# Attention context in 64-column tiles with whole transposes, in a fused language-model tower on one core

## The chip, the cores and the metric

The kernel runs on one core of a Trainium2 chip. The core's engines are TensorE (PE; its weight loads are listed apart as PEld), VectorE (DVE), ScalarE (ACT), GpSimd (POOL) and the DMA queues, here fed by SyncE (SP). The metric is the device time of one execution in microseconds (us), the median of several runs. Lower is better.

## The reference

Sixteen sequences of 128 tokens go through one transformer layer. A token adds only its bracket level (0 to 31) to the model, so a row of the input is one of 32 rows of a table:

```python
levels = _compute_levels(token_ids, 32)         # scan with clip over 128 tokens
h = level_emb[levels] * 0.15                    # 16 x 128 x 256
x = layernorm(h)
q = x @ Wq + bq          # 16 heads of 16
k, v = x @ Wk + bk, x @ Wv + bv                 # 4 key heads, repeated 4 times
attn = softmax(q @ k.T / 4)                     # no mask
h = h + (attn @ v) @ Wo + bo
...
Wq1, Wq2 = quantize(W1), quantize(W2)           # ternary: clip(round(W / mean|W|), -1, 1)
h = h + relu(layernorm(h) @ Wq1.T + b1) @ Wq2.T + b2     # 1024 hidden columns
```

## The kernel before, in words

Two rows of one sequence with the same level are equal, so everything is computed once for each of 32 levels in each of 16 sequences: 512 rows, as four **groups** g = 0 to 3 of four sequences (4 x 32 = 128 rows). Which level occurs how often in a sequence weights the softmax. In the names, `BG` is 4 (sequences in a group), `H2` is 2, `D` 256, `KVD` 64 and `VW` 68 (64 value columns and 4 columns for the sums of the four key heads).

The stages are these.

1. The levels: tokens are compared, a scan (`level_scan`) makes levels, `level_ends`, `end_codes` and `gone_levels` find the highest and lowest level of each sequence, `end_columns` (line 623, tile `endx`) spreads them for a matmul, `level_onehot` makes the one-hot `oh`.
2. Scores of the table: keys (`ktm`, split in a rounded part `khi` and a rest `klo`) and queries (`qs`, written by `query_hi` on ACT and `query_lo` on DVE). `scores` (lines 949, 950) makes the 128 x 128 table of scores; `prefix_max` (two scans), `prefix_t` (line 955, two transposes), `maxima`, `max_hi` and `max_parts` (tile `ms`) make from it the row maxima of each sequence. `scores_t(g)` writes the transposed scores of group g into its PSUM bank `psg[g]`, and `less_max` (line 980, 16 matmuls) subtracts the maxima.
3. Attention: `exps(g)` on ACT makes `et`; `values` on DVE makes `vo`, and POOL multiplies it by the counts to `voc`, one instruction a group (line 392). `context(g)` (line 988): four matmuls, one a sequence, each with 128 columns of `et` as weights and 68 columns of `voc` moving. The 128 columns are the four query heads of a key head by 32 levels, in two halves `a` of 64. `inverse_sums(g)` and `normalise(g)` divide (`cn`, DVE). `context_t(g)` (line 997): sixteen small transposes of 64 x 64 pieces as eight matmuls against an identity. `ctx_out(g)` copies them to `cT` (ACT), `out_proj(g)` (line 1006) multiplies by Wo, `add_table(g)` adds the residual (`hq`).
4. The second layernorm: `row_stats`, `row_moments`, `variance_eps` (DVE), a power on POOL (line 400) for two groups at once, `norm_rows` (ACT), `rows_t` (line 1012, two transposes a group), `x_hi` (ACT) and `x_lo` (DVE), which split in a rounded part and a rest.
5. Feed-forward: the weights are made ternary on the way: `magnitudes(w, i)` (ACT, line 442) and `signs(w, i)` (DVE, line 703, and one quarter on POOL, line 386), a sum on PE (`abs_total`), `threshold(w)`, `ternary(w, q)` (DVE, line 720), `weights_t(u)` (PE, line 1046) and `weights_out(u)` (ACT). `ffn1(h, j)` (line 1064, four matmuls of 256 columns) makes 128 hidden columns j of the two groups of half h; `hidden` (ACT) and `hidden_lo` (DVE) apply relu and split; `ffn2(j, g)` (line 1079, two matmuls) adds them up for group g; `final(g)`, `spread(g)` (line 1098), `result(g)` and the output DMAs follow.

Every engine runs a list of such steps that is written out by hand, and waits on semaphores; there is no scheduler. `keep_warm(n)` (line 884) are n matmuls of zeroes that only fill TensorE's time. SP issues all loads at the start in one order, and the outputs at the end.

The order of the lists is what ties the engines together. On PE before:

```python
less_max()
keep_warm(5, psmisc[0])
weights_t(0)
context(0)
context(1)
context_t(0)
weights_t(1)
context_t(1)
out_proj(0)
out_proj(1)
```

## Time and profile before

| | |
|---|---|
| median of 3 runs | 58.94 us (58.08 to 59.61) |
| the profiled execution | 58.45 us |
| its span, first to last instruction | 56.6 us |
| granted TensorE clock, mean over the span | 0.975 |
| PE busy | 49.2 us (87%), 416 records |
| DVE busy | 42.0 us (74%) |
| ACT busy | 31.2 us (55%) |
| POOL busy | 19.8 us (35%) |

A matmul of 32-bit type in its full precision stands as two records in the trace, and so do its weight loads. A busy PE is not PE at its peak: records overlap, so the pace is read from one start to the next and not from the durations. The profiled execution lasts 1.85 us longer than its span.

### The profile page before, as it was taken

How to read it: one execution, taken by the hardware profiler on the slowest of the kernel's cores; microseconds unless marked ns; L12 is line 12 of the kernel's file. 1: busy time of each engine (PE TensorE's matmuls, PEld its weight loads, DVE VectorE, ACT ScalarE, POOL GpSimd, SP SyncE). 2: the span in 40 equal slices, each digit the busy share in tenths (PEclk: the TensorE clock that was granted, in tenths of full speed). 3: DMA queues.
4: the chain of work that ended last, by engine and by line, in shares of the span. 5: the costliest groups of instructions: out<-in, count | busy, mean ns of one | idle time of the engine just before them, and what ended most of it. 6: DMA issues, size and time to landing. Idle time of an engine off the chain costs nothing.

```text
span 56.6 us, 1236 instructions
## 1 busy us (share of the span) xinstructions
PE 49.2 (87%) x416; PEld 38.7 (68%) x416; DVE 42.0 (74%) x140; ACT 31.2 (55%) x73; POOL 19.8 (35%) x36
## 2 busy tenths in 40 slices
PE   1999999899996969996699999999999999998300
PEld 0333797546875958895479899989999688994000
DVE  4998739999699999699199987955659599347400
ACT  0585007832129916950980897989796958106100
POOL 5935089998049920009900000695000000000000
PEclk9999999999999999999999999999999999999955
DMA  0363899986520000000000000000000009730594
GB/s 0 67 204 55 159 260 411 417 333 148 131 76 12 12 0 0 0 0 0 0 12 0 0 0 0 0 0 0 6 0 0 12 5 364 255 116 0 210 383 148
DMA packets 4658, 5.37 MB, mean 95 GB/s; under 512 B 1117, under 2 KB 4141, under 8 KB 4653
## 3 DMA queue, kind: packets, MB, share of 16 engines
q1 hardware_dynamic: 4602, 5.28, 29.3%
q8 instruction: 3, 0.05, 0.3%
q10 hardware_dynamic: 51, 0.02, 0.1%
q14 instruction: 2, 0.02, 0.1%
HBM read 3.21 MB, written 2.10 MB: 94 GB/s over the span
## 4 chain that ended last, share of the span: by engine, by line
PE 66%; DVE 16%; issue 5%; ACT 3%; POOL 2%; DVEq 0%; POOLq 0%
PE pswt L1064 15%; PE psmisc L1079 14%; PE psg L880 6%; PE psg L1006 5%; DVE tern L720 5%; PE psg L1098 5%; PE psg L997 4%; PE psg L1012 3%; PE psg L884 2%; PE psg L1046 2%; POOL rs L400 2%; PE psg L967 2%; DVE hq L744 1%; DVE st L748 1%; PE psg L972 1%
## 5 line engine op out<-in xcount | busy, mean ns | idle before, releaser
L478 ACT ACTIVATE hr<-pswt,b1c 128x256 f32<-128x256 f32 x16 | 7.6, 473 | 2.8 <-PE pswt L1064 2.5
L1079 PE MATMUL psmisc<-w2T,hh 128*128 128x256 f32 x32 | 8.4, 292 | 0.0
L1079 PE MATMUL psmisc<-w2T,hl 128*128 128x256 f32 x32 | 8.0, 281 | 0.0
L1064 PE MATMUL pswt<-xhi,w1T 128*128 128x256 f32 x32 | 7.1, 303 | 0.0
L771 DVE TENSOR_TENSOR hl<-hr,hh 128x256 fp32r<-128x256 f32 x16 | 6.4, 424 | 0.7 <-ACT hh L480 0.3
L720 DVE SCALAR_TENSOR_TENSOR tern<-aw,thr,sg 128x512 bf16<-128x512 f32 x8 | 6.5, 842 | 0.0
L1064 PE MATMUL pswt<-xlo,w1T 128*128 128x256 f32 x32 | 6.4, 281 | 0.0
L1079 PEld LDWEIGHTS psmisc<-w2T,hh 128*128 128x128 f32 x32 | 6.1, 190 | 0.3 <-DVE hl L771 0.3
L400 POOL TENSOR_TENSOR rs<-ve,mhalf 128x2 f32<-128x2 f32 x2 | 1.7, 871 | 12.6 <-DVE ve L756 12.6
L1079 PEld LDWEIGHTS psmisc<-w2T,hl 128*128 128x128 f32 x32 | 6.1, 190 | 0.0
L1064 PEld LDWEIGHTS pswt<-xhi,w1T 128*128 128x128 f32 x32 | 5.0, 190 | 0.6 <-ACT hr L478 0.3
L1064 PEld LDWEIGHTS pswt<-xlo,w1T 128*128 128x128 f32 x32 | 4.9, 189 | 0.0
L392 POOL TENSOR_TENSOR voc<-vo,cpos 128x272 f32<-128x272 f32 x4 | 3.8, 966 | 2.5 <-DVE vo L694 2.5
L880 PE MATMUL psg<-warm 128*128 128x512 bf16 x8 | 3.6, 631 | 1.2 <-DVE tiny L547 1.2
L442 ACT ACTIVATE aw<-w 128x1024 f32<-128x1024 f32 x4 | 4.2, 1053 | 0.2 <-DMA w<-in_L_ffn_W_dram 0.2
L1006 PE MATMUL psg<-wo,cT 128*128 128x256 f32 x16 | 4.2, 392 | 0.0
L485 ACT ACTIVATE aw<-psg 128x256 f32<-128x256 f32 x6 | 2.0, 384 | 3.9 <-PE psg L1098 3.9
L988 PE MATMUL psg<-voc,et 128*128 128x68 f32 x32 | 4.0, 274 | 0.0
L988 PEld LDWEIGHTS psg<-voc,et 128*128 128x128 f32 x32 | 3.8, 192 | 0.0
L386 POOL TENSOR_SCALAR sg<-w 128x1024 bf16<-128x1024 f32 x1 | 3.6, 3642 | 0.0
L776 DVE TENSOR_TENSOR fin<-psmisc,hb 128x256 f32<-128x256 f32 x4 | 1.7, 423 | 2.5 <-PE psmisc L1079 2.5
L781 DVE COPY aw<-psg 128x256 f32<-128x256 f32 x7 | 2.7, 420 | 1.1 <-PE psg L1098 1.1
(166 smaller groups left out, 114.5 us busy)
## 6 DMA issues: line engine op xcount, KB each, us to landing
w<-in_L_ffn_W_dram SPq DMA_DIRECT2D x4, 512.0 KB, 6.0
out_dram<-aw SPq DMA_DIRECT2D x8, 256.0 KB, 2.3
wq<-in_L_attn_Wq_dram SPq DMA_DIRECT2D x1, 256.0 KB, 3.1
wo<-in_L_attn_Wo_dram SPq DMA_DIRECT2D x4, 64.0 KB
emb<-in_L_tok_level_emb_dram SPq DMA_DIRECT2D x1, 128.0 KB
bo_bc<-in_L_attn_bo_dram SPq DMA_DIRECT2D x1, 128.0 KB, 8.3
b_bc<-in_L_ffn_b_dram SPq DMA_DIRECT2D x1, 128.0 KB, 7.0
wk<-in_L_attn_Wk_dram SPq DMA_DIRECT2D x1, 64.0 KB, 2.4
```

Source lines behind the costliest of these rows:

```text
L386: nc.gpsimd.tensor_scalar(sg[:, 0, 0:1024], halves(0, 0), 0.0, 0.5, ALU.is_ge, ALU.subtract).then_inc(g_sgn, 1)
L392: nc.gpsimd.tensor_tensor(voc[:, bs, :], vo[:].unsqueeze(1).to_broadcast([P, BG, VW]), cpos[:, bs].unsqueeze(2).to_broadcast([P, BG, VW]), ...
L400: nc.gpsimd.tensor_tensor(rs2[:, c], ve2[:, c], mhalf[:].to_broadcast([P, HALF]), ALU.pow).then_inc(g_rs2, 1)
L442: nc.scalar.activation(aw[:, w, i * 1024:(i + 1) * 1024], halves(w, i), ACT.Abs, accum_out=asum[:, 2 * w + i:2 * w + i + 1]).then_inc(a_ab ...
L478: nc.scalar.activation(hr[:, n % NHR, :], pswt[n % 2][:, 0:RH], ACT.Relu, bias=b1c[:, j:j + 1]).then_inc(a_hr, 1)
L720: V.scalar_tensor_tensor(tern[:, w, c], aw[:, w, c], thr[:, w:w + 1], sg[:, w, c], ALU.is_gt, ALU.mult).then_inc(v_tern, 1)
L771: V.tensor_tensor(hl[:, n, :], hr[:, n % NHR, :], hh[:, n, :].bitcast(F32), ALU.subtract).then_inc(v_hl, 1)
L880: mm(bank[:, :], warm[:, 0:P], warm[:], start=True, stop=True)
L988: ins = mm(psg[g][:, b * VW:(b + 1) * VW], et[:, g, b, :], voc[:, g * BG + b, :], start=True, stop=True)
L1006: ins = mm(psg[g][:, 0:D], cT[:, g, e].rearrange("p b l -> p (b l)"), wo[:, e, :], start=(e == 0), stop=(e == H2 - 1))
L1064: ins = mm(pswt[n % 2][:, 0:RH], w1T[:, j, k, :], part[:, k, HALF * h:HALF * (h + 1), :].rearrange("p g n -> p (g n)"), start=(m == 0 and ...
L1079: ins = mm(psmisc[r][:, 0:D], part[:, n, r * P:(r + 1) * P], w2T[:, j, :], start=(j == 0 and m == 0), stop=(j == FC - 1 and m == 1))
```

## The change

There are three parts.

- `context(g)` makes the context of two sequences together: the weights are 64 columns of `et` (half `a` of one sequence), and the output of the two sequences t = 0, 1 of a pair goes to partitions 0 to 63 and 64 to 127 of the same columns. Eight matmuls a group in place of four, each with half of the weight columns and again 68 moving columns. The sums and the product by their inverse (`inverse_sums`, `normalise`) are as before.
- With this layout, `context_t(g)` is two whole 128 x 128 transposes in place of eight matmuls on 64 x 64 pieces, and `ctx_out(g)` reorders while it copies.
- The lists of PE, DVE and ACT have a new order. POOL's and SP's are the same.

```diff
             def ctx_out(g):
                 act.wait_ge(p_cT, g + 1)
-                nc.scalar.activation(cT[:, g].rearrange("p e b l -> p (e b l)"), psg[g][:, 0:D], ACT.Copy).then_inc(a_cT, 1)
+                nc.scalar.activation(cT[:, g], psg[g][:, 0:D].rearrange("p (b e l) -> p e b l", b=BG, e=H2), ACT.Copy).then_inc(a_cT, 1)
...
             def context(g):
                 pe.wait_ge(g_voc, g + 1)
                 pe.wait_ge(a_exp, g + 1)
-                for b in range(BG):
-                    ins = mm(psg[g][:, b * VW:(b + 1) * VW], et[:, g, b, :], voc[:, g * BG + b, :], start=True, stop=True)
+                for pair in range(H2):
+                    for a in range(2):
+                        c = (2 * pair + a) * VW
+                        for t in range(2):
+                            b = 2 * pair + t
+                            ins = mm(psg[g][64 * t:64 * t + 64, c:c + VW], et[:, g, b, 64 * a:64 * a + 64], voc[:, g * BG + b, :],
+                                     start=True, stop=True)
                 ins.then_inc(p_ctx, 1)
 
             def context_t(g):
                 pe.wait_ge(v_cn, g + 1)
-                dst = psg[g][:, 0:D].rearrange("p (e b l) -> p b e l", e=H2, b=BG)
-                for b in range(BG):
-                    for a in range(2):
-                        q = slice(64 * a, 64 * a + 64)
-                        ins = mm(dst[q, b], cn[q, g, b * KVD:(b + 1) * KVD], identf[q, q], start=True, stop=True)
+                for pair in range(H2):
+                    ins = nc.tensor.transpose(psg[g][:, pair * P:(pair + 1) * P], cn[:, g, pair * P:(pair + 1) * P], identf[:])
                 ins.then_inc(p_cT, 1)
```

Of the lists the diff shows two places on PE; `keep_warm` matmuls go from 27 to 22.

```diff
             less_max()
-            keep_warm(5, psmisc[0])
             weights_t(0)
+            abs_total(1)
             context(0)
             context(1)
+            context(2)
             context_t(0)
```

Three places are shown as they stand in the programs. First, **DVE from the keys to the prefix maxima**, in the first quarter. Before, from `key_blocks` (`ktm`) on:

```order
L637 SCALAR_TENSOR_TENSOR ktm<-psmisc,bkc,km 128x128
L628 TENSOR_SCALAR above<-jlev,ends 16x128
L631 SCALAR_TENSOR_TENSOR gone<-jlev,ends,above 16x128
L616 SCALAR_TENSOR_TENSOR ends<-ends 16x1 x2
L643 CAST khi<-ktm 128x128
L653 TENSOR_TENSOR qs<-psg,qs 64x2x32
L647 TENSOR_TENSOR klo<-ktm,khi 128x128
L653 TENSOR_TENSOR qs<-psg,qs 64x2x32
L623 TENSOR_SCALAR endx<-sele,ends 16x128 x2
L660 TENSOR_SCALAR oh<-pswt,pnum 128x256
L683 SCALAR_TENSOR_TENSOR pmx<-reset,psmisc 128x128
L660 TENSOR_SCALAR oh<-pswt,pnum 128x256
```

After, from `gone_levels` (`above`) on:

```order
L628 TENSOR_SCALAR above<-jlev,ends 16x128
L631 SCALAR_TENSOR_TENSOR gone<-jlev,ends,above 16x128
L637 SCALAR_TENSOR_TENSOR ktm<-psmisc,bkc,km 128x128
L623 TENSOR_SCALAR endx<-sele,ends 16x128 x2
L643 CAST khi<-ktm 128x128
L653 TENSOR_TENSOR qs<-psg,qs 64x2x32 x2
L647 TENSOR_TENSOR klo<-ktm,khi 128x128
L660 TENSOR_SCALAR oh<-pswt,pnum 128x256
L675 SCALAR_TENSOR_TENSOR top<-pswt,pnum,bm 128x128
L660 TENSOR_SCALAR oh<-pswt,pnum 128x256
L683 SCALAR_TENSOR_TENSOR pmx<-reset,psmisc 128x128 x2
```

`gone_levels` and the end codes move ahead of the keys, `endx` moves from behind `klo` and `qs` to ahead of `khi`, and both scans (`pmx`) follow each other, where the second stood one row below the piece shown and `oh` between them.

Second, **DVE from the maxima to the first two contexts**. Before:

```order
L699 SCALAR_TENSOR_TENSOR ms<-mhi,lowrow,psmisc 128x128
L707 TENSOR_SCALAR gam<-pswt 128x2
L710 TENSOR_TENSOR thr<-gam 128x1
L690 COPY cpos<-pswt 128x16
L691 TENSOR_TENSOR vo<-pswt,bm 128x64
L694 COPY vo<-bm 128x4
L720 SCALAR_TENSOR_TENSOR tern<-aw,thr,sg 128x512
L686 TENSOR_SCALAR ident<-ridx 128x128
L720 SCALAR_TENSOR_TENSOR tern<-aw,thr,sg 128x512 x2
L725 RECIPROCAL rec<-psg 128x16
L730 TENSOR_TENSOR cn<-psg,rec 128x256
```

After:

```order
L720 SCALAR_TENSOR_TENSOR tern<-aw,thr,sg 128x512
L699 SCALAR_TENSOR_TENSOR ms<-mhi,lowrow,psmisc 128x128
L690 COPY cpos<-pswt 128x16
L691 TENSOR_TENSOR vo<-pswt,bm 128x64
L694 COPY vo<-bm 128x4
L686 TENSOR_SCALAR ident<-ridx 128x128
L703 TENSOR_SCALAR sg<-w 128x1024
L720 SCALAR_TENSOR_TENSOR tern<-aw,thr,sg 128x512 x2
L725 RECIPROCAL rec<-psg 128x16
L707 TENSOR_SCALAR gam<-psmisc 128x2
L710 TENSOR_TENSOR thr<-gam 128x1
L730 TENSOR_TENSOR cn<-psg,rec 128x256
```

The first ternary (`tern`) moves ahead of `ms`; `sg` of the second weights stands between the identity and the next two ternaries, and the second threshold (`gam`, `thr`) and `eb` stand among the normalisations.

Third, **PE up to the first feed-forward matmul**, from the third context before and from the fourth one after. Before:

```order
L988 MATMUL psg<-voc,et 128x68 x4
L1021 MATMUL psmisc<-asum,ones 128x2
L1046 MATMUL pswt<-ident,tern 128x128 x4
L884 MATMUL psmisc<-warm 128x256
L988 MATMUL psg<-voc,et 128x68 x4
L1012 MATMUL psg<-identf,xn 128x128 x2
L997 MATMUL psg<-identf,cn 64x2x32 x8
L1012 MATMUL psg<-identf,xn 128x128 x2
L997 MATMUL psg<-identf,cn 64x2x32 x8
L1006 MATMUL psg<-wo,cT 128x256 x2
L1064 MATMUL pswt<-xhi,w1T 128x256 x2
```

After:

```order
L992 MATMUL psg<-voc,et 64x68 x8
L999 MATMUL psg<-identf,cn 128x128 x2
L1048 MATMUL pswt<-ident,tern 128x128 x8
L1008 MATMUL psg<-wo,cT 128x256 x2
L999 MATMUL psg<-identf,cn 128x128 x2
L1048 MATMUL pswt<-ident,tern 128x128 x4
L884 MATMUL psmisc<-warm 128x256
L1014 MATMUL psg<-identf,xn 128x128 x4
L1008 MATMUL psg<-wo,cT 128x256 x2
L884 MATMUL psmisc<-warm 128x256 x2
L1066 MATMUL pswt<-xhi,w1T 128x256 x2
```

`context(2)` now stands ahead of this place. The transposes of groups 2 and 3 (L997, now L999) and the product by Wo of group 2 (L1006, now L1008) move ahead of the normalised rows (L1012, now L1014); that of group 3, which stood among the feed-forward matmuls, stands right behind them.

Among the ACT steps, `magnitudes(1, 0)` moves ahead of `max_hi` and `magnitudes(1, 1)` ahead of the exponentials; both stood behind them.

## Rows read from the trace of the kernel before

**Rows 1.** The page: busy time, share of the span and instructions of each engine.

```profile
PE 49.2 (87%) x416; PEld 38.7 (68%) x416; DVE 42.0 (74%) x140; ACT 31.2 (55%) x73; POOL 19.8 (35%) x36
```

**Rows 2.** Stretch 30.50 to 50.80: busy time (x instructions) of each engine, PEclk, DMA.

```profile
30.50:50.80 20.30, 20.30 (x175) 18.56 (x173) 14.73 (x44) 14.67 (x36) 3.10 (x5) 1.00 0.15 53
```

**Rows 3.** The chain that ended last: start us, us, what.

```profile
11.50 0.23 PE psg L967
...
15.43 0.35 DVE ms L699
...
19.88 0.43 DVE cn L730
...
24.45 0.38 DVE st L748
...
25.08 0.16 DVE ve L756
...
33.48 0.86 PE psg L1006 x4
...
50.76 0.68 PE psg L1098 x8
```

**Rows 4.** Timeline 7.9 to 12: start us, us, engine line op [idle before <-releaser].

```profile
7.95 0.35 DVE L637 SCALAR_TENSOR_TENSOR ktm<-psmisc,bkc,km 128x128 f32<-128x128 f32 x1 [1.22 <-issue]
8.21 2.06 POOL L382 TENSOR_SCALAR sel<-jdx,pnum 128x512 fp32r<-128x512 int32 x1
...
9.15 0.21 DVE L643 CAST khi<-ktm 128x128 fp32r<-128x128 f32 x1
...
9.97 0.23 DVE L653 TENSOR_TENSOR qs<-psg,qs 64x64 fp32r<-64x64 f32 x1
10.25 3.64 POOL L386 TENSOR_SCALAR sg<-w 128x1024 bf16<-128x1024 f32 x1
10.34 0.30 PE L949 MATMUL psmisc<-khi,qs 128*128 128x128 f32 x1 [0.28 <-DVE qs L653]
...
11.52 0.48 DVE L660 TENSOR_SCALAR oh<-pswt,pnum 128x256 fp32r<-128x256 f32 x1
```

**Rows 5.** Line 623, both instructions: duration ns min/median/max.

```profile
L623 DVE TENSOR_SCALAR endx<-sele,ends x2: 234/666/1099, 10.2 to 11.2; 16x128 bf16<-16x128 bf16 x2
```

**Rows 6.** Timeline of TensorE at the prefix transposes.

```profile
13.12 0.38 PE L955 MATMUL psmisc<-identf,pmx 128*128 128x128 f32 x2
```

**Rows 7.** Tile w, the feed-forward weights: durations ns min/median/max; time to landing.

```profile
L442 ACT ACTIVATE aw<-w x4: 1047/1053/1060, 9.3 to 22.3; 128x1024 f32<-128x1024 f32 x4
...
DMA to landing us min/median/max: 4.6/6.0/7.1
```

**Rows 8.** Timeline of TensorE, VectorE and GpSimd, 15.8 to 20.4.

```profile
15.89 0.67 PE L980 MATMUL psg<-ms,sel 32*128 32x128 f32 x16
16.24 0.74 DVE L720 SCALAR_TENSOR_TENSOR tern<-aw,thr,sg 128x512 bf16<-128x512 f32 x1
16.42 3.75 POOL L392 TENSOR_TENSOR voc<-vo,cpos 128x272 f32<-128x272 f32 x4 [2.53 <-DVE vo L694]
...
17.49 2.19 DVE L720 SCALAR_TENSOR_TENSOR tern<-aw,thr,sg 128x512 bf16<-128x512 f32 x2
17.89 1.95 PE L988 MATMUL psg<-voc,et 128*128 128x68 f32 x16
...
20.36 0.68 PE L997 MATMUL psg<-identf,cn 64*64 64x64 f32 x16 [0.52 <-DVE cn L730]
```

**Rows 9.** Timeline of GpSimd: the two power instructions.

```profile
25.38 1.04 POOL L400 TENSOR_TENSOR rs<-ve,mhalf 128x2 f32<-128x2 f32 x1 [5.20 <-DVE ve L756]
...
35.75 0.70 POOL L400 TENSOR_TENSOR rs<-ve,mhalf 128x2 f32<-128x2 f32 x1 [7.37 <-DVE ve L756]
```

**Rows 10.** Timeline of TensorE at the first normalised rows.

```profile
27.46 0.44 PE L1012 MATMUL psg<-identf,xn 128*128 128x128 f32 x2 [1.08 <-ACT xn L464]
...
30.20 0.59 PE L1064 MATMUL pswt<-xhi,w1T 128*128 128x256 f32 x2
```

175 lines of the change are left out of this document (87 added, 88 removed).

## The prediction

> **What bounds the kernel now.** I read the page first. TensorE (PE) is busy for 49.2 of 56.6 us and DVE for 42.0 [rows 1]. That is an average, so I went on to single stretches. From 30.5 to 50.8 us PE has no idle time at all, while DVE and ACT are busy for 14.7 us of the 20.3 [rows 2]: this is feed-forward work that stands in PE's queue, and only less of it or an earlier start shortens it. The chain of waits agrees: it reaches the last spreads at 50.76 over PE alone [rows 3]. Before 30 us the chain changes engines. It goes over the row maxima (`ms`, 15.43), the ternaries, the first context divided (`cn`, 19.88) and the moments of the second layernorm (`ve`, 25.08) to the normalised rows on PE at 27.46, before which PE stood idle for 1.08 us [rows 3, 10]. So there are two currencies. What comes off DVE's chain before 25.2 makes the feed-forward start earlier, and what comes off PE's queue behind 27.46 makes it start earlier or last less. Work taken off PE before that is worth only what waits for it.
>
> **The new matmuls.** Two old contexts are 16 records in 1.95 us [rows 8]. A record lasts 0.27 (two transposes 0.11 apart take 0.38 [rows 6]), so starts are (1.95 - 0.27) / 15 = 0.112 apart, 0.9 us for the 8 of a group. With only 68 moving columns the load of 128 weight columns can be what sets this pace. The new form has 16 records of half the weights for each group. The nearest row is the old transpose: 64 x 64 pieces with 64 moving columns, 16 records a group in 0.68 us, by the same reading 0.03 apart, 0.46 a group [rows 8]. Bounds for a new context are therefore 0.46 us (pairs run together), 0.9 (half the load, no pairs) and 1.8 (each record as slow as now). I take 0.5, since the row with the same weight columns and nearly the same moving columns shows it. For contexts 0 to 2 this hardly counts: POOL makes one `voc` in 0.94 us on average, four in 3.75 [rows 8], and each context must wait for its own. Two whole transposes, 0.11 apart, are 0.22 and replace 0.46, so 0.25 is saved a group, 1.0 us in all, 0.5 of it (groups 2 and 3) in the stretch behind 27.46 where PE's queue counts. But there the steps move as well, so I don't count it twice.
>
> The Trainium skill (TensorEngine Tiling (Array Packing), section Theoretical Speedup) gives up to twice the rate where the weights have no more than 64 columns. By it a context is half of today's 0.9, about the lower bound; the trace has no 128 x 64 tiles to say.
>
> **Step 1, to the scores.** DVE stands idle for 1.22 us before `ktm` at 7.95, and `above` to `ends`, 0.94 us from 8.21 to 9.15, stand between `ktm` and `khi` [rows 4]. They now fill the gap. Both `endx` come ahead of `khi`. They took 1.10 and 0.23 us [rows 5] and lay behind `klo`; I take 0.5 for the two, since the long one started with POOL's `sg` at 10.25 and now falls 2 us earlier; 0.3 and 1.3 are the ends. Scores started at 10.34 [rows 4], now at 10.34 - 0.94 + 0.5 = 9.9. On PE the two `keep_warm` ahead of the level matmul are hidden, because the scan behind it waits for DVE's own `norm_table`.
>
> **Step 2, to the prefix transposes.** They started at 13.12 [rows 6]. Behind the scores DVE now has `oh`, `top`, `oh` and two scans, without `endx`: 0.40 for an `oh` (11.52 to 11.92) [rows 4], by the same reading 0.26 for `top` and 0.33 a scan, so 10.0 + 1.7 = 11.75. PE's two `scores_t`, three records of 0.23 each [rows 3], end at about the same time. The transposes start at 11.85, 1.25 earlier.
>
> **Step 3, to `less_max`.** It started at 15.89 [rows 8], 2.77 behind the transposes. Now a third `scores_t` (0.7) stands between on PE, a ternary (0.7) between on DVE, and a pass of magnitudes (1.05) between on ACT, whose data is there (the four loads land 4.6 to 7.1 us after their issue around 5) [rows 7]. The first two run beside each other; the third ends at 13.7, when the maxima are ready. So 11.85 + 2.77 + 0.7 = 15.35, and `ms` ends at 15.1 instead of 15.7. Of the 1.25 won, 0.55 is left; the rest has paid for work that is gone later.
>
> **Step 4, to `cn`.** Here POOL and DVE take turns. A ternary took 0.74 us alone at 16.24, and two took 2.19 beside `voc` [rows 8], 1.05 to 1.1 each. Now DVE has, from 15.1: `values` 0.3, identity 0.3, `sg` 1.1 (the price of a ternary in turns), two ternaries 2.15, the inverse 0.28, the second threshold 0.26, `cn` 0.42. That gives 19.85, against 20.30 before. `sg` and the threshold cost 1.4 of chain here; the ternary ahead of `ms` and an earlier `ms` pay for it.
>
> **Step 5, to `ve`.** Behind `cn` come 0.95 for an inverse, `eb` and the second `cn`; then inverse 0.25, ternary 0.7, `cn` 0.40 (as the statistics of 256 columns, 0.38 [rows 3]) and `sg` 0.60: DVE is free at 22.7. The product by Wo of group 0 starts on PE at 21.1 and takes 0.86 [rows 3], so it doesn't set this. Two sums with the table, their statistics and one more inverse are 2.1: 24.8, against 25.24. POOL's power took 1.04 us at 25.38 beside DVE's `sg`, and 0.70 later [rows 9]; a ternary now starts beside it, so I leave 1.04. Rows are normalised on PE at 27.46 - 0.45 = 27.0.
>
> A rule of the Trainium skill (SBUF — State Buffer, section SBUF: two separate sides) says that a GpSimd instruction and certain VectorE ones exclude each other for the whole instruction. The rows of `voc` and of the power look like this. But `khi` ran in 0.21 inside POOL's `sel` of 2.06 us, and `endx` (1.10) came through long before `sg` (3.64) ended [rows 4, 5]. By the rule the front would lose 1.7 us (C below).
>
> **Step 6, to the first feed-forward matmul.** Before, 2.74 us lay between 27.46 and 30.20 [rows 10]: two groups of rows, two old transposes, one product by Wo. Now it is 0.5 for the second row's normalisation, 0.26 for its transposes, 0.1 until ACT has copied the context of group 3, 0.86 for the product and 0.23 for two `keep_warm`, 1.95 in all. The start is 28.95, 1.25 earlier.
>
> **Step 7, the feed-forward.** From 30.20 to the first spread of the last half PE's work was 20.5. The product by Wo of group 3 (0.86) and two `keep_warm` (0.23) have left it. I walked the new order against ACT and DVE: `ffn2(2, 1)` waits some 0.4 for `hidden_lo`, other waits are below 0.1. I add 0.3. The last spreads, copies and DMAs, 5.9 us from 50.76, are unchanged.
>
> **The sum.** 1.25 + 1.09 - 0.3 = 2.05 us off. The profiled execution goes from 58.45 to 56.4, its span from 56.6 to 54.55. Off the median of 58.94 this is **56.9 us**.
>
> **Rivals.** (A) *DVE's chain gives nothing.* If `endx` meets `sel` as it met `sg` (1.3 in place of 0.5) and `voc` with three DVE neighbours goes slower by a few tenths, `ve` is at 25.6 to 25.9 and the feed-forward starts at 29.75 to 30.05. Then little more than the 0.8 of step 7 is left: 57.8. For it: ternaries of 1.05. Against: 1.2 us of idle time that is really there.
>
> (B) *The feed-forward gives it back.* DVE and ACT have 5.6 us free in 20.3 [rows 2]. A denser PE needs `hidden_lo` earlier, `rows_t(2)` and `rows_t(3)` stand together behind twelve `ffn2`, and ACT holds `norm_rows(2)` ahead of a `hidden`. One such wait of 1.0 us at the normalised rows gives 57.9.
>
> (C) *`endx` waits for `sel` to its end.* Started at 8.25, the first would end only behind `sel`'s end at 10.27 and the second at 10.5 instead of 8.75, so all the rest comes 1.7 later: 58.6. `khi` inside `sel` speaks against it [rows 4].
>
> That is what the rule of the whole instruction in the Trainium skill (SBUF — State Buffer) would do here.
>
> (D) *The context is slower, and the kernel too.* If a record with 64 weight columns keeps the old pace of 0.112, a group takes 1.8 us. Contexts 0 to 2 would then hold PE from 16.75 (1.4 behind `less_max`) to 22.15, in front of the first transpose, which otherwise goes at 19.9: 2.25 late, and 1.3 more at context 3, so 56.9 + 3.5 = 60.4. It decides from 1.4 us a group on, where 3 x 1.4 - 3.1 + 0.9 eats the 2.0; below 0.94 POOL hides most of it. The small tiles' 0.03 a record speak against it [rows 8]. A fall of TensorE's clock would end on the same side: before, it was full from 30.5 to 50.8 [rows 2], and between 17 and 21 us PE now does less, since five `keep_warm` and half the context's time are gone.
>
> That the change doesn't do what it says is a small case: that the tiles don't run in pairs but load in half the time (0.9 a group) would cost 0.4 at most, and is in the forecast's range.
>
> **How the numbers follow.** A measurement of this kernel tells about 2%, 1.2 us, from no change: faster is below 57.76. My forecast has 0.50 (56.2 to 57.4), A 0.20 (57.4 to 58.2), B 0.12, C 0.04, D with the clock 0.09; 0.05 is for more than 2.7 us off, if the turns with POOL are shorter than I take them. Faster by over 2%: 0.50 + 0.05 + 0.07 of A and B = 0.62. Slower: 0.09. Within: 0.29. For 8 in 10 the range goes from 55.9 to 58.4: it takes in the forecast's own range, half of the surprise below it, A and most of B.
>
> **What would show it.** Right: line 992's 16 records of a group start within 0.5 us, the prefix transposes start near 11.9, `less_max` near 15.4, `rows_t` at 27.0 and `ffn1` at 28.9, PE without idle time from there to the spread near 48.6. Wrong: an `endx` above 1 us ahead of `khi`, `less_max` at 15.9 or later (A or C), gaps of PE in the feed-forward before L1081 (B), a pace of 0.1 at L992 or a PEclk below 1 before the end (D).

## The result and the profile after

The changed kernel takes 55.92 us (median of 4 runs, 55.77 to 56.2); the kernel before, run beside it, 59.27 us (58.08 to 62.96). The ratio is 0.9624, 95% interval 0.9562 to 0.9685, so the change is faster by 3.8%. Executions whose time lies more than 1.5% above the fastest of the same kernel are left out of every ratio, here and below; among those of the kernel before they raise the median, so times of different batches are compared by ratio. The profiled execution went from 58.45 to 56.2 us, its span from 56.6 to 54.4.

The page of the changed kernel has fewer records on PE (387 instead of 416) and nearly the same shares as [rows 1]:

```profile
PE 47.4 (87%) x387; PEld 35.6 (65%) x387; DVE 40.6 (75%) x140; ACT 30.7 (56%) x73; POOL 20.4 (37%) x36
```

The window of the feed-forward part, from the first L1066 to the last spread, is the one to compare with [rows 2]. Columns are the stretch, its length, busy time (x instructions) of PE, PEld, DVE, ACT and POOL, then PEclk, DMA share and GB/s:

```profile
29.18:48.53 19.35, 19.33 (x170) 17.68 (x168) 13.67 (x42) 14.13 (x35) 2.83 (x5) 1.00 0.14 48
```

PE is busy for 19.33 of 19.35 us, and DVE and ACT still have more than 5 us free. Before, the same part lasted 20.56 us, from 30.20 to 50.76 [rows 3, 10].

The chain of waits, at the places that answer to [rows 3] (start us, us, what):

```profile
15.87 0.34 DVE ms L699
...
19.77 0.41 DVE cn L730
...
24.62 0.13 DVE ve L756
...
28.16 0.96 PE psg L1008 x4
...
48.53 0.68 PE psg L1100 x8
```

`ms` and the first `cn` stand at about their old times (+0.44, -0.11), `ve` comes 0.46 us earlier, the last spread 2.23. So up to the first division the front gave 0.11 us in this execution, and most of the rest came late in the program. The timeline from 5.4 to 16.4 us says why the front gave little. The rows answer to [rows 4, 5, 6]; columns are start, duration, engine, line, operation, and in brackets the idle time before it with what ended it:

```profile
5.44 1.46 PE L884 MATMUL psg<-warm 128*128 128x256 bf16 x6
...
8.08 0.63 PE L910 MATMUL psmisc<-xT,wk 128*128 128x32 f32 x4
8.81 0.35 DVE L637 SCALAR_TENSOR_TENSOR ktm<-psmisc,bkc,km 128x128 f32<-128x128 f32 x1 [1.26 <-PE psmisc L910]
9.08 0.40 DVE L623 TENSOR_SCALAR endx<-sele,ends 16x128 bf16<-16x128 bf16 x2
9.40 0.21 DVE L643 CAST khi<-ktm 128x128 fp32r<-128x128 f32 x1
...
10.94 0.33 PE L949 MATMUL psmisc<-khi,qs 128*128 128x128 f32 x1
...
12.66 0.55 PE L955 MATMUL psmisc<-identf,pmx 128*128 128x128 f32 x2
...
16.32 0.67 PE L980 MATMUL psg<-ms,sel 32*128 32x128 f32 x16
```

Both `endx` take 0.40 us together and disturb nobody, as Step 1 had it. But `ktm` now starts at 8.81 where it was at 7.95 before, and DVE had been idle for 1.26 us until PE's keys (L910) came. Scores start 0.60 us later than before, and still the prefix transposes start 0.46 us earlier.

The middle of the kernel, answering to [rows 8, 9, 10]:

```profile
16.55 0.69 DVE L703 TENSOR_SCALAR sg<-w 128x1024 bf16<-128x1024 f32 x1
16.59 3.83 POOL L392 TENSOR_TENSOR voc<-vo,cpos 128x272 f32<-128x272 f32 x4 [2.40 <-DVE vo L694]
...
17.79 0.69 PE L992 MATMUL psg<-voc,et 128*64 128x68 f32 x16 [0.30 <-POOL voc L392]
...
20.51 0.44 PE L999 MATMUL psg<-identf,cn 128*128 128x128 f32 x2
...
24.88 1.12 POOL L400 TENSOR_TENSOR rs<-ve,mhalf 128x2 f32<-128x2 f32 x1 [4.46 <-DVE ve L756]
...
27.23 0.93 PE L1014 MATMUL psg<-identf,xn 128*128 128x128 f32 x4 [0.65 <-ACT xn L464]
...
29.18 0.48 PE L1066 MATMUL pswt<-xhi,w1T 128*128 128x256 f32 x2
```

A context of 16 records starts and ends within 0.69 us, and a pair of whole transposes takes 0.44 to its end; two old contexts took 1.95 us and sixteen small transpose records 0.68 [rows 8].

### The profile page after: what moved, and what is told of

Same layout as the page of the kernel before. It is cut to its first block, busy times and chain, and to the rows that moved or that the text cites. A ratio compares the mean times of both kernels' runs of the same rounds, so it can differ in the third digit from the quotient of the medians.

```text
span 54.4 us, 1178 instructions
## 1 busy us (share of the span) xinstructions
PE 47.4 (87%) x387; PEld 35.6 (65%) x387; DVE 40.6 (75%) x140; ACT 30.7 (56%) x73; POOL 20.4 (37%) x36
## 4 chain that ended last, share of the span: by engine, by line
PE 66%; DVE 17%; issue 4%; ACT 3%; POOL 3%; DVEq 0%; POOLq 0%
PE pswt L1066 15%; PE psmisc L1081 15%; PE psg L880 7%; PE psg L884 6%; PE psg L1100 5%; DVE tern L720 4%; DVE sg L703 2%; POOL rs L400 2%; PE psg L1048 2%; ACT xn L464 2%; PE psg L1014 2%; PE psg L1008 2%; PE psg L923 2%; DVE cn L730 2%; DVE st L748 1%
## 5 line engine op out<-in xcount | busy, mean ns | idle before, releaser
L1066 PE MATMUL pswt<-xhi,w1T 128*128 128x256 f32 x32 | 6.8, 295 | 0.0
L1066 PE MATMUL pswt<-xlo,w1T 128*128 128x256 f32 x32 | 6.4, 281 | 0.0
L1066 PEld LDWEIGHTS pswt<-xhi,w1T 128*128 128x128 f32 x32 | 4.9, 189 | 0.8 <-issue 0.3
L1066 PEld LDWEIGHTS pswt<-xlo,w1T 128*128 128x128 f32 x32 | 4.9, 189 | 0.0
L1008 PE MATMUL psg<-wo,cT 128*128 128x256 f32 x16 | 4.2, 398 | 0.0
L460 ACT ACTIVATE cT<-psg 128x256 f32<-128x256 f32 x4 | 1.5, 378 | 4.1 <-PE psg L999 4.1
L884 PE MATMUL psg<-warm 128*128 128x256 bf16 x19 | 3.8, 335 | 0.0
L767 DVE CAST hh<-hr 128x256 fp32r<-128x256 f32 x9 | 2.5, 282 | 1.7 <-ACT hr L478 1.6
L992 PE MATMUL psg<-voc,et 128*64 128x68 f32 x64 | 2.8, 229 | 1.0 <-POOL voc L392 1.0
```

The costliest lines, as they stand in the source:

```text
L884: mm(bank[:, 0:256], warm[:, 0:P], warm[:, 0:256], start=True, stop=True)
L1008: ins = mm(psg[g][:, 0:D], cT[:, g, e].rearrange("p b l -> p (b l)"), wo[:, e, :], start=(e == 0), stop=(e == H2 - 1))
L1066: ins = mm(pswt[n % 2][:, 0:RH], w1T[:, j, k, :], part[:, k, HALF * h:HALF * (h + 1), :].rearrange("p g n -> p (g n)"), start=(m == 0 and ...
```

## The experiments

Eleven variants ran, and the changed kernel once more (after_again). A further one, ctx_one_tile, in which the second sequence of a pair overwrites the first, gave no time; ctx_low_tile asks its question. They are told in the order of the questions that they answer. This table has the moments of the profiled execution of each that matter (us from the span's start; keys are L910, scores L949, prefix L955, `ve` the second of the first pair, rows `rows_t(0)`; "warm" is how long the last six `keep_warm` ahead of `table_t` take together, seven or eight where it is marked).

| kernel | warm | keys | scores | prefix | less_max | ve | rows | first ffn1 | last spread | span |
|---|---|---|---|---|---|---|---|---|---|---|
| before | 1.44 (x7) | 7.29 | 10.34 | 13.12 | 15.89 | 25.08 | 27.46 | 30.20 | 50.76 | 56.6 |
| changed | 1.46 | 8.08 | 10.94 | 12.66 | 16.32 | 24.61 | 27.23 | 29.18 | 48.53 | 54.4 |
| after_again | 1.43 | 7.94 | 10.80 | 12.52 | 16.18 | 24.46 | 27.08 | 29.03 | 48.38 | 54.3 |
| layout_only | 1.36 (x7) | 7.21 | 10.52 | 13.30 | 16.01 | 24.56 | 26.94 | 29.39 | 49.86 | 55.8 |
| sg_behind | 0.83 | 7.05 | 9.91 | 11.63 | 15.30 | 23.75 | 26.38 | 28.34 | 47.68 | 53.6 |
| mags_late | 1.03 | 7.54 | 10.40 | 12.11 | 15.78 | 24.07 | 26.36 | 28.25 | 47.60 | 53.5 |
| both | 0.87 | 7.14 | 9.94 | 11.65 | 15.37 | 23.72 | 26.32 | 28.27 | 47.62 | 53.5 |
| kw_behind | 1.05 (x8) | 6.82 | 10.51 | 13.52 | 17.30 | 25.57 | 28.19 | 30.15 | 49.49 | 55.4 |
| tern_behind | 0.83 | 6.82 | 10.51 | 13.36 | 17.30 | 25.58 | 28.18 | 30.14 | 49.48 | 55.4 |
| wo3_late | 1.46 | 7.97 | 10.83 | 12.55 | 16.21 | 24.50 | 27.12 | 29.07 | 50.99 | 56.9 |

### Which part of the change pays: layout_only, order_only, after_again

The first kernel is the one before with the new `context`, `context_t` and `ctx_out` and its old lists; the second has the new lists with the three old functions; the third is the changed kernel once more, on the same chip.

```diff
 layout_only: the three functions of the change in the lists of before
 order_only:  the lists of the change with the three functions of before
```

> The kernel before with its own lists, and only the new context, the whole transposes and the reordering copy. My account: at the first two contexts DVE's ternaries are late anyway, so only the shorter transposes count there (about 0.4 us); behind the first normalised rows the transposes of groups 2 and 3 save 0.25 each. Together 0.9 us faster than before, a ratio of 0.985. If the layout carried the change, it would be 2 us or more (0.965); if a context were hidden entirely and only PE's idle time grew, 0 to 0.3 us (0.995 or more). The records of one context start within 0.5 us in each case.

> The changed kernel's lists with the context and the small transposes of before. My account: contexts 0 and 1 hide behind POOL's products, the third ends 0.45 us later, the transposes cost 0.25 a group; the sum with the table of group 0 comes 0.4 to 0.6 us later and PE's idle time ahead of the normalised rows takes the rest. So 0.5 us slower than the changed kernel, 1.7 faster than before: ratio 0.97. If the gain was the layout, it is 0.99 to 1.0; if layout and order don't need each other at all, 0.962.

> The changed kernel once more, for the same chip and for a second profile. The ratio is 0.962 within its interval. The question is the front: in its first profile TensorE's clock rose at 7.1 us instead of 6.1, and the scores started at 10.94. If the late rise is chance, this profile can show the rise at another time, and the scores nearer to 10.3; if it comes from the list, it is 7.1 again.

Measured: layout alone 57.58 us, ratio 0.9852 (0.9757 to 0.9946); order alone 0.9643 (0.9532 to 0.9753), which rests on two executions, 55.96 and 56.15, of six from 55.96 to 59.58; both, the changed kernel again, 55.43 us, 0.9515 (0.9426 to 0.9604). In microseconds of the 58.6 that the kernel before took there, the parts are 0.9 (0.3 to 1.4) and 2.1 (1.4 to 2.7), and the whole is 2.8 (2.3 to 3.4). So each part pays by itself, and they add up as well as these intervals can tell; that one helps or hinders the other by something under 1 us is not excluded.

Where the layout's 0.9 us come from can be read in layout_only's timeline:

```profile
18.10 1.17 PE L992 MATMUL psg<-voc,et 128*64 128x68 f32 x32
...
20.48 0.44 PE L999 MATMUL psg<-identf,cn 128*128 128x128 f32 x2 [1.21 <-DVE cn L730]
...
21.39 1.99 PE L1008 MATMUL psg<-wo,cT 128*128 128x256 f32 x8
...
22.56 0.42 DVE L744 TENSOR_TENSOR hq<-psg,eb 128x256 f32<-128x256 f32 x1
...
26.94 0.44 PE L1014 MATMUL psg<-identf,xn 128*128 128x128 f32 x2 [1.42 <-ACT xn L464]
...
29.39 0.48 PE L1066 MATMUL pswt<-xhi,w1T 128*128 128x256 f32 x2
```

Before, DVE had stood idle for 0.56 us until the product by Wo, which started at 21.91, let `hq` start at 23.08. Now two whole transposes have ended sooner, the product starts at 21.39, `hq` at 22.56 without a wait, and `ve` is 0.52 us earlier though `less_max` was 0.12 later. From the first rows (26.94) to the first feed-forward matmul 2.45 us pass instead of 2.74, with two groups' transposes between. In the old lists, then, the layout shortened a wait of DVE on PE ahead of `ve` that my sum did not count. What did it are the whole transposes: behind the faster contexts PE stood idle for 1.21 us until the first `cn`, and for 1.42 us ahead of the rows. So here the contexts' own pace was worth little or nothing.

The order's share is where Steps 6 and 7 put it: from layout_only to after_again the stretch from the rows to `ffn1` goes from 2.45 to 1.95 us, the feed-forward part from 20.47 to 19.35. That is 1.6 us together.

The profiled execution of order_only doesn't show the order's worth, since TensorE's clock fell in it:

```profile
19.93:26.76 6.83, 6.83 (x49) 5.87 (x48) 3.38 (x9) 1.25 (x3) 0.14 (x1) 0.50 0.00 0
```

Three groups of old contexts follow each other in it from 17.44 on and take 3.73 us, but the last of them runs into the fall, so the two that precede it (17.44 to 19.60) are all that can be set beside the 1.95 us for two before. From 16.00 to 19.93, ahead of the fall, PE was busy for 3.63 of 3.93 us. The mean granted clock of its six executions was 0.93 to 1.0. In the eight executions of the changed kernel, with the same lists, the mean granted clock was 0.97 to 1.0, and in the two that were profiled it did not fall between the scores and the last spread, so rival D stayed away. Whether the new contexts keep the clock up in these lists, or whether it was chance, is not shown.

### What the context's pace comes from: ctx_unpaired, ctx_low_tile

In the changed kernel neighbours in PE's queue use different tiles (partitions 0 to 63, 64 to 127). ctx_unpaired changes the nesting, so that two matmuls of a tile follow each other:

```diff
-                    for a in range(2):
-                        c = (2 * pair + a) * VW
-                        for t in range(2):
-                            b = 2 * pair + t
+                    for t in range(2):
+                        b = 2 * pair + t
+                        for a in range(2):
+                            c = (2 * pair + a) * VW
```

> The changed kernel, with the eight matmuls of a context in another order: both halves of the first sequence of a pair, then both of the second, so that the two matmuls that use the same 64 columns of the array follow each other. If the pace of 0.03 us a record comes from two tiles at work side by side, it rises to about 0.045 to 0.06 between records (0.7 to 0.95 us a context), with hardly a change of the time, since POOL sets the pace (0 to 0.3 us slower than the changed kernel). If it comes from the smaller weights alone, the pace stays at 0.03.

Measured: 0.9633 (0.9554 to 0.9713), on the chip where the changed kernel gave 0.9515. A group's 16 records take 0.74 us instead of 0.69, and they still start two by two, 0.013 apart instead of 0.007. So the pace hardly changed. That left both causes standing, fewer weight columns or two tiles beside each other: PE could still overlap neighbouring pairs. ctx_low_tile settles it with eight matmuls in a row on one tile:

```diff
-                for pair in range(H2):
-                    for a in range(2):
-                        c = (2 * pair + a) * VW
-                        for t in range(2):
+                for t, u in ((1, 0), (0, 0), (1, 1)):
+                    for pair in range(H2):
+                        for a in range(2):
+                            c = (2 * pair + a) * VW
                             b = 2 * pair + t
-                            ins = mm(psg[g][64 * t:64 * t + 64, c:c + VW], ...
+                            ins = mm(psg[g][64 * u:64 * u + 64, c:c + VW], ...
```

> The changed kernel with one edit in the context: the matmuls of the second sequences of the two pairs are first written to partitions 0 to 63, then those of the first sequences to the same place (these stay), then those of the second sequences again to partitions 64 to 127 (these stay too). So a group has twelve matmuls, 24 records, of which the first 16 all use the lower tile and no two neighbours use different tiles; the result is that of the changed kernel. In the changed kernel 16 records of alternating tiles start within 0.47 us, 0.03 apart. If a record takes 0.03 because the two tiles run beside each other, one tile alone goes at 0.06, and the first 16 records start within 0.9 us, all 24 in 1.4. If it takes 0.03 because half the weight columns are loaded, 24 records start within 0.7 us. I expect the second, since the pace in the kernel with the tiles not alternating stayed the same. The time of the kernel says little: contexts 0 to 2 wait for POOL anyway, so 0.1 to 0.8 us more than the changed kernel.

Measured: 56.38 us in the profiled execution, span 54.6 (a second run 57.1). Its contexts in the timeline, and the two kinds of instruction of line 992 (duration ns min/median/max, first and last start us):

```profile
23.17 1.46 PE L992 MATMUL psg<-voc,et 128*64 128x68 f32 x24
```

```profile
L992 PEld LDWEIGHTS psg<-voc,et x96: 132/137/137, 16.8 to 24.3; 128*64 128x64 f32 x96
L992 PE MATMUL psg<-voc,et x96: 222/223/274, 16.8 to 24.4; 128*64 128x68 f32 x96
```

The 24 records of a group take 1.46 us, what I had written for one tile at 0.06 a record. Record by record it is plain. From the second on they start 0.059 us apart (16.941, 17.000, 17.060, 17.119 ...). Then one starts 0.006 behind another (17.592, 17.598), and from there two rows of starts run beside each other, each at 0.059 (17.651, 17.710, 17.770 and 17.709, 17.768, 17.827). The trace does not name the tile of a record; the counts, 16 in the first row and 8 in the second, are those of the lower and of the upper tile. So 64 weight columns instead of 128 halve the time from one start to the next, from 0.112 to 0.059, and two tiles beside each other halve it again to 0.03. I expected the first of these to be all. Two matmuls of a tile in a row, as in ctx_unpaired, are still overlapped with the next two; eight are not. A group has twice as many records as before, 16 for 8, so the first halving only pays for the split: on one tile 16 records at 0.059 are 0.94 us, by the old form 8 at 0.112 are 0.90. What a group gained, it gained from the second tile.

The Trainium skill (TensorEngine Tiling (Array Packing), Theoretical Speedup) gives up to twice the rate where a dimension of the matmul is at most 64. The starts of 0.059 and 0.03 agree with it.

At 1.46 us a group the contexts are also no longer hidden behind POOL: 72 records run without a gap from 16.84 on, DVE waits for them ahead of the inverses, and from `less_max` to the first `ffn1` it is 13.99 us instead of 12.86 (15.38 to 29.37; 16.32 to 29.18). That is rival D's mechanism shown at a price: 1.13 us for contexts of 1.46 us, in one profiled execution.

### Why the front gave less: both, kw_behind, sg_behind

In the changed kernel `query_bias` stands between `table_t` and the keys, and drops and warm matmuls stand in another order ahead of them. kw_behind gathers the warm matmuls behind `drops`, to find which comes first; `both` puts the bias back ahead of `table_t` (and the ternary behind `normalise(3)`, as in tern_behind below).

```diff
 kw_behind:
-            keep_warm(2, psg[0])
             drops()
-            keep_warm(6, psg[0])
+            keep_warm(8, psg[0])
 both:
+            query_bias()
             table_t()
             keep_warm(4, psg[0])
-            query_bias()
             keys()
```

> The changed kernel with the two warming matmuls that stand ahead of the level matmul put behind it (8 in a row there, none ahead). Before the result I held that they are hidden, since the level scan waits for DVE's own work: then the time is that of the changed kernel (0.962, within 0.005). If the later start of the table's transposes behind them costs the front 0.2 to 0.4 us that reaches the end, it is 0.955 to 0.96.

> The kernel of the run before, and besides the bias matmul of the queries ahead of the table's transposes, as before the change, no longer between them and the keys. At the same start of TensorE's full clock the keys come 0.2 us earlier (the bias took 0.36 there, and what it takes ahead of the transposes is partly waiting for the normalised table), and the front up to the row maxima with them. Together with the ternary 0.4 to 0.6 us faster than the changed kernel. If the front is bound by DVE and not by PE, only 0.2 to 0.4 as in the run before.

Measured for kw_behind: 57.14 us in three of four runs, 55.66 in the other. No ratio follows. In the profiled one full clock came early, the eight warm matmuls took 1.05 us and the keys started at 6.82, but the clock was down again from 10.75 to 14.16 us, so that `less_max` came at 17.30. It shows what else can hold up the front. `klo` took 1.08 us instead of 0.29, since it started 0.10 us behind POOL's `sg`:

```profile
9.28 3.64 POOL L386 TENSOR_SCALAR sg<-w 128x1024 bf16<-128x1024 f32 x1
9.38 1.08 DVE L647 TENSOR_TENSOR klo<-ktm,khi 128x128 fp32r<-128x128 f32 x1
...
10.51 0.33 PE L949 MATMUL psmisc<-khi,qs 128*128 128x128 f32 x1 [0.75 <-DVE klo L647]
```

This is not the edit's doing: tern_behind, whose front is the changed kernel's, had the same moments in its profiled execution (keys 6.82, `klo` 9.38 for 1.08 us, scores 10.51, the clock down from 10.94 to 14.35). Nor does every early front run into `sg`: in sg_behind (below) the keys started at 7.05, `klo` 0.22 us ahead of `sg`, and it took 0.29. So whether moving the two warm matmuls costs anything stays open.

Measured for both: 55.31 us, 0.952 (0.9464 to 0.9575). Its front:

```profile
5.44 0.87 PE L884 MATMUL psg<-warm 128*128 128x256 bf16 x6
...
7.14 0.56 PE L910 MATMUL psmisc<-xT,wk 128*128 128x32 f32 x4
7.81 0.35 DVE L637 SCALAR_TENSOR_TENSOR ktm<-psmisc,bkc,km 128x128 f32<-128x128 f32 x1 [0.19 <-PE psmisc L910]
...
9.94 0.33 PE L949 MATMUL psmisc<-khi,qs 128*128 128x128 f32 x1
```

DVE waits 0.19 us for the keys and not 1.26, and the scores start 1.0 us earlier than in the changed kernel. But only a part is the edit's. Six warm matmuls took 0.87 us here and 1.46 in the changed kernel, because full clock came 1.6 us later there; in sg_behind, whose front is the changed one, they took 0.83 and the scores started at 9.91. The fair partner is mags_late, which has the changed front and where the warm matmuls took 1.03: its scores are at 10.40, so the edit is worth 10.40 - 9.94 less 0.16 of warm matmuls, 0.3 us. The other 0.7 us are the moment at which TensorE goes to full clock, which differs between executions of the same list: after_again has the changed kernel's own list and every moment 0.14 us earlier.

From keys to scores PE needs 2.86 us in each of the executions with the changed front that kept their clock (8.08 to 10.94, 7.94 to 10.80, 7.54 to 10.40, 7.05 to 9.91), with no idle time. It goes on so to `less_max`. The two rows are the changed kernel and the kernel before, from the keys to `less_max`:

```profile
8.08:16.32 8.24, 8.24 (x55) 5.78 (x54) 6.70 (x23) 5.36 (x12) 6.12 (x3) 1.00 0.75 267
```

```profile
7.29:15.89 8.60, 8.32 (x56) 5.79 (x55) 7.16 (x24) 3.40 (x8) 6.60 (x4) 1.00 0.83 277
```

PE is busy for all of the 8.24 us. Before, it had 0.28 us of idle time in 8.60, and that is nearly all that a new order of DVE could take out of this stretch. The scores hang on PE's queue and no longer on DVE, and so does `less_max`. Seven `keep_warm` between keys and scores take 0.97 us of that queue (9.44 to 10.08, 10.29 to 10.62), so here they no longer fill idle time. What leaving them out would give was not tried; `klo` ends 0.25 us ahead of the scores and is the next limit.

sg_behind is about the other end of the front. It moves `signs(1, 0)` from the place ahead of the two ternaries to behind `normalise(1)`:

```diff
             identities()
-            signs(1, 0)
             ternary(0, 1)
...
             normalise(1)
+            signs(1, 0)
             inverse_sums(2)
```

> The changed kernel with the second weights' first signs behind the second division instead of ahead of two ternaries. I priced them at 1.1 us in turns with POOL; the profile shows 0.60. Behind the division they cost 0.6 as well, but the first division comes 0.6 earlier, and so does the first transpose; the sum with the table comes only when DVE is free, at the same time. So the same time as the changed kernel (0.962, within 0.005). If the first division is the step that everything waits for, it is 0.6 us faster (0.952).

Measured: 55.58 us, 0.9532 (0.947 to 0.9594). The first `cn` starts 3.05 us behind `less_max` instead of 3.45, but `ve` starts 8.45 behind it instead of 8.29. The 0.4 us are paid back before `ve`: in the changed kernel DVE is busy for 8.21 of the 8.29 us between `less_max` and `ve`, so behind the division `sg` costs its 0.6 us again. Here DVE has one wait of 0.25 us, for the first context. The place of this `sg` is worth nothing.

### Where endx must stand: endx_behind

```diff
-            end_columns()
             key_hi()
             query_lo(0)
             query_lo(1)
             key_lo()
+            end_columns()
```

> The changed kernel with the spreading of the level ends behind the rests of keys and queries on DVE, as before. In the changed kernel's profile it took 0.40 for both and lay in DVE's idle time, since the queries are what is late. Then moving it back makes the front later: it collides with POOL's signs (1.1 us as before) and stands ahead of the one-hots; the prefix transposes come 0.7 to 1.2 us later, of which 0 to 0.7 reaches the end (0.962 to 0.975). If it was on the path ahead of the keys, the time falls by 0.3 us (0.957).

Measured: 60.03 us (58.45 to 60.34). The fastest of the four, 58.45, stands with the kernel before on that chip (57.96 to 58.5 in six of seven executions), so the whole gain is gone; that it is slower than before is not shown. The front:

```profile
10.52 3.67 POOL L386 TENSOR_SCALAR sg<-w 128x1024 bf16<-128x1024 f32 x1
10.60 1.18 DVE L623 TENSOR_SCALAR endx<-sele,ends 16x128 bf16<-16x128 bf16 x2
11.84 0.28 PE L930 MATMUL pswt<-endx,ones 16*128 16x256 bf16 x1 [1.70 <-DVE endx L623]
...
12.71 0.33 PE L949 MATMUL psmisc<-khi,qs 128*128 128x128 f32 x1
```

```profile
14.02:20.85 6.83, 6.83 (x24) 4.49 (x22) 4.47 (x17) 2.73 (x6) 0.75 (x2) 0.50 0.14 39
```

With `endx` behind `klo` the two instructions meet POOL's `sg` and take 1.18 us instead of 0.40. In the new list of PE the matmul L930 (`level_ends`), which reads `endx`, stands ahead of the scores, so PE stood idle for 1.70 us and the scores started at 12.71 instead of 10.94. Behind that the clock was down from 14.02 to 20.85 us; before it fell PE had been busy for 5.12 of 6.82 us. The prefix transposes start 2.1 us later (14.77), where 0.7 to 1.2 was expected: the expectation had not counted that PE's list waits for L930. The place of `endx` is worth 1.8 us at the scores; how much of the rest the clock took and how much the late scores was not separated.

### The magnitudes and the ternary ahead of the last cn: mags_late, tern_behind

mags_late moves two passes of magnitudes on ACT from around `max_hi` to behind `weights_out(0)` and `ctx_out(1)`, with `threshold(1)` and `abs_total(1)` later to match. tern_behind swaps two steps of DVE.

```diff
 mags_late, ACT:
-            magnitudes(1, 0)
             max_hi()
-            magnitudes(1, 1)
...
             weights_out(0)
+            magnitudes(1, 0)
             ctx_out(0)
             ctx_out(1)
+            magnitudes(1, 1)
 tern_behind, DVE:
             variance_eps(1)
-            ternary(1, 0)
             normalise(3)
+            ternary(1, 0)
```

> The changed kernel with the magnitudes of the second weights where they stood before on ACT (behind the weights' first copy and behind the second context's copy), with their sum on PE behind the fourth context and their threshold on DVE behind the variances. The exponentials don't wait for them in either case. My account: the early place fills ACT's idle time in the front and costs nothing there; in the late place ACT delays the copy of the third context and the normalised rows little, since it has 1.9 and 2.0 us of idle time there. So 0 to 0.4 us slower than the changed kernel (0.962 to 0.969). If the early place makes the maxima late (they were rounded at 14.69, 0.2 us after the pass ended), the late place is 0.2 to 0.4 us faster.

> The changed kernel with one step moved on DVE: the division of group 3 now stands ahead of the first ternary of the second weights, and no longer behind it. In the changed kernel POOL's power took 1.12 us beside that ternary; in the kernel with the late magnitudes, where the ternary started 0.18 us behind the power, 0.73. So here the power takes 0.73 again, the normalised rows are transposed 0.4 us earlier behind the variances, and the time falls by 0.2 to 0.4 us. If the 1.12 has another cause, power and time stay.

Measured: mags_late 55.5 us, 0.9451 (0.9344 to 0.9559); tern_behind 56.09 us, 0.9621 (0.9558 to 0.9684). In mags_late `less_max` is still 3.67 us behind the prefix transposes, 3.66 in the changed kernel, so the pass of 1.05 us ahead of `mhi` was hidden. What it gains is behind `ve`: the rows follow it by 2.29 us instead of 2.62. In tern_behind they follow by 2.60 although the power is as short as in mags_late:

```profile
25.86 0.72 POOL L400 TENSOR_TENSOR rs<-ve,mhalf 128x2 f32<-128x2 f32 x1 [4.46 <-DVE ve L756]
26.68 1.06 POOL L404 TENSOR_SCALAR mr<-mv,rs 128x1 f32<-128x1 f32 x2
```

```profile
24.34 0.73 POOL L400 TENSOR_TENSOR rs<-ve,mhalf 128x2 f32<-128x2 f32 x1 [4.46 <-DVE ve L756]
25.17 0.50 POOL L404 TENSOR_SCALAR mr<-mv,rs 128x1 f32<-128x1 f32 x2
```

In the changed kernel the power takes 1.12 us and the mean times it 0.68, and in tern_behind 0.72 and 1.06. The swap moved the long time from the first of POOL's instructions to the second, which starts 0.02 us ahead of the second ternary (26.70); the sum stays at 1.8. In mags_late the ternary starts 0.18 us behind the power (in the changed kernel 0.22 ahead of it), and the two take 1.23 in all. That a ternary at the wrong moment is the cause fits all three, but it was not isolated. mags_late's interval overlaps with that of after_again, and so do those of `both` and sg_behind: none of them is shown to be faster than the changed kernel. The three edits together were not tried.

### The product by Wo: wo3_late

```diff
             rows_t(1)
-            out_proj(3)
             keep_warm(2, psmisc[0])
...
             ffn1(0, 3)
+            out_proj(3)
             ffn2(0, 0)
```

> The changed kernel with the product by Wo of group 3 back among the feed-forward matmuls, behind the fourth ffn1. By my account of the gain it stands ahead of the feed-forward in a place where PE otherwise waits (for ACT to split the normalised rows), so that it costs 0.5 us less there. Moved back, the first ffn1 starts 0.3 to 0.6 us earlier (it then waits for the rests of the rows, x_lo), and the rest of the queue is 0.86 longer: 0.3 to 0.6 us slower than the changed kernel at the same start of TensorE's full clock. If the place doesn't matter, since PE's queue is full on both sides, the time is the same within 0.1 us.

Measured: 58.57 us (12 runs), 1.0058 (1.0014 to 1.0101). In these lists the product alone, put back where it stood before, takes away the whole gain. Its timeline:

```profile
29.07 0.47 PE L1066 MATMUL pswt<-xhi,w1T 128*128 128x256 f32 x2 [0.81 <-ACT w1T L450]
...
31.64 1.03 PE L1008 MATMUL psg<-wo,cT 128*128 128x256 f32 x4
32.71 0.42 DVE L744 TENSOR_TENSOR hq<-psg,eb 128x256 f32<-128x256 f32 x1 [2.78 <-PE psg L1008]
...
33.84 0.39 PE L1081 MATMUL psmisc<-w2T,hh 128*128 128x256 f32 x1 [1.18 <-DVE hl L771]
```

Two things happen. The first `ffn1` comes at 29.07, no earlier than the 29.03 of after_again, whose `less_max` (16.18 for 16.21) is the same, since it then waits 0.81 us for its weights (`w1T`, ACT): the product had stood in a place that was free on PE. It was expected 0.3 to 0.6 us earlier, and the whole 0.3 to 0.6 us slower. And in DVE's new list the sum of group 3 stands ahead of the first `hl`, so DVE waits 2.78 us for the product, and the first `ffn2` 1.18 us for `hl`. The last spread is at 50.99 against 48.38 in after_again. So the 2.6 us are not the price of the product: 0.86 is its own time in the queue, and the waits that DVE's list makes of it are the rest. The product's move with DVE's list put back too was not tried.

## Why the prediction was right, and where it was not

Predicted were 56.9 us, 2.05 less than 58.94, which is 3.5%; measured are 3.8% (3.2 to 4.4), and 2.25 us between the two profiled executions, 2.2 between their spans. The number on the clock, 55.92, lies 0.98 lower than predicted mostly because the sum was taken off 58.94: the ratio sets 58.10 (55.92 / 0.9624) against it, 0.84 less. That the change itself came out within 0.2 us is in part luck, as the steps show.

- **The new matmuls.** Right in size: starts 0.03 apart, 16 records starting within 0.47 us where 0.46 to 0.5 was predicted. The reason given, the old transposes' row, was two effects in one (fewer columns, two tiles), as ctx_low_tile shows. The case that I called small, half the load and no pairs at 0.9 a group, was not run. Of the 1.0 us that the shorter transposes were to save, layout_only shows about 0.8: 0.52 ahead of `ve`, which the sum did not have, and 0.29 behind the rows.
- **Step 1, the scores at 9.9.** Wrong by 1.04 us in this execution, and by 0.5 in mags_late (10.40), where the warm matmuls ended as early as in the kernel before. I worked the scores out from DVE alone and looked on PE only at the two `keep_warm` ahead of the level matmul. The step that failed is the sentence that PE's part is hidden: `query_bias` between `table_t` and the keys and the queue of 2.86 us behind the keys bind the scores now. PE had only 0.28 us of idle time between keys and `less_max` to begin with, so DVE's free 1.22 us ahead of `ktm` were no measure of the gain. `endx` at 0.40 was right (0.5 predicted), and 9.91 was reached when full clock came early (sg_behind).
- **Step 2, the transposes.** The stretch from the scores is 1.72 us where 1.95 was predicted and 2.78 stood before. `endx` has left it, but so has one of PE's three `scores_t`, which stands behind the transposes now: of the 1.06 us, Step 3 gives back 0.89. From keys to `less_max` the gain is 0.36 us (8.60 to 8.24).
- **Step 3, less_max.** 3.66 behind the transposes, 3.5 predicted, 2.77 before; PE has no idle time in it, and taking ACT's pass out (mags_late) left it at 3.67. With Step 1's error it comes at 16.32 and not at 15.35.
- **Step 4, cn.** From the end of `ms` (16.21) to the end of `cn` (20.18) are 3.97 us; I had written 4.75 (my terms add up to 4.81, and by [rows 3] `ms` ended at 15.78 before and not at 15.7). The term that was too large is DVE beside `voc`: `sg` took 0.60 of chain, not 1.1, and the identity 0.13, not 0.3. This `sg` started 0.04 us ahead of `voc` and was not held. These 0.8 us cancelled most of Step 1's error.
- **Step 5, ve and the rows.** From the end of `cn` to the end of `ve` are 4.57 us, 4.95 predicted, so the last of Step 1's error is gone: `ve` ends at 24.75 (24.8 predicted). The power takes 1.12 (1.04), and the rows are on PE at 27.23 (27.0).
- **Step 6.** The rows to `ffn1` take 1.95 us, the value predicted; the start is at 29.18 for 28.95. Right, but not a free move: wo3_late shows that it holds in these lists together with DVE's order, and that the product costs no time there, as it fills PE's wait for the weights.
- **Step 7.** 20.56 became 19.35, so 1.21 us came off, where 1.09 less 0.3 of stalls was predicted. The wait of `ffn2(2, 1)` did not come; PE's idle time in the whole part is 0.02 us. So rival B is out.
- **The sum.** 1.02 ahead of the first `ffn1` (1.25 predicted) and 1.21 behind (0.79). The total came out closer than its parts: 0.23 too much ahead, 0.42 too little behind, and within the front the larger pair of Steps 1 and 4. That these errors cancelled was luck.
- **Rivals.** A is out: beside `sel` the two `endx` took 0.40 and not 1.3, and two ternaries beside `voc` 2.18 as before (2.19). C is out for the same reason, since both `endx` ran within POOL's `sel` of 2.01 us (8.55 to 10.56). D stayed away in the changed kernel, but each half of it was seen elsewhere: slower contexts in ctx_low_tile, a fall of the clock in order_only, kw_behind, tern_behind and endx_behind. The last but one has the changed kernel's own front, so such a fall is not shown to come from an edit. D's price was twice too high: by its sum, contexts of 1.46 us cost 2.2 (3 x 1.46 - 3.1 + 0.96), and 1.13 was measured.

On C, the rule of the Trainium skill (SBUF — State Buffer, SBUF: two separate sides) that the pair is held for the whole instruction is not what most of these rows show: a DVE instruction that started at about the same time as POOL's `sg` of 3.64 us was held until 1.1 to 1.2 us behind its start, and two inside `sel` were not held. One case fits the rule, DVE's `sg` at the end of POOL's (last section).

## What to carry to other kernels

When steps leave an engine's chain in front of a shared consumer, walk the consumer's own queue with the same care: here PE, not DVE, set the scores after the change, since it had 0.28 us of idle time from keys to `less_max` before, and one small matmul in the wrong place cost 0.3 us. Matmuls that fill idle time belong to that queue too; whether the seven of them here cost time now was not tried. A move in one engine's list can be worth nothing or the whole gain depending on the lists of the others, so undo it alone before believing its term. Cutting a small matmul into two of half the columns pays only where the two halves use different tiles and neighbours in the queue: on one tile the doubled count ate the halved time (0.94 us for 0.90), on two it left 0.47. And it pays only where something waits for the matmul; in the old lists the transposes that the new layout allowed were what counted.
